# Level 5 of a blockwise inverse in 32x32 tiles of TensorE, its neighbour in column tiles, and a new order of one superstep

## The reference

```python
def step(S, inputs):
    q_t, k_t, v_t, g_t, b_t = inputs
    S = S * jnp.exp(g_t)[..., None]
    kv = jnp.einsum('bhd,bhdv->bhv', k_t, S)
    delta = b_t[..., None] * (v_t - kv)
    S = S + k_t[..., None] * delta[:, :, None, :]
    o = jnp.einsum('bhd,bhdv->bhv', q_t, S)
    return (S, o)
```

## Time and profile before

| what | value |
|---|---|
| median of 3 runs | 5065.29 us (5062.55 to 5066.39) |
| the profiled execution's own time | 5056.96 us |
| its span | 5055.0 us |
| granted TensorE clock, mean | 0.992 |
| TensorE busy | 4725.1 us (93%) |
| VectorE, ScalarE, GpSimd busy | 3754.1, 3339.2, 2881.8 us |

### The profile page before, as it was taken

The page is one execution under the profiler, slowest core; times in us unless marked ns, Lnnn a source line. Parts: engine busy times, 40 slices in busy tenths (PEclk is TensorE's granted clock), DMA queues, the critical chain, the costliest instruction groups (busy, mean ns, idle before and its releaser), DMA issues.

```text
span 5055.0 us, 111131 instructions
## 1 busy us (share of the span) xinstructions
PE 4725.1 (93%) x28928; PEld 3607.3 (71%) x28928; DVE 3754.1 (74%) x8897; ACT 3339.2 (66%) x7216; POOL 2881.8 (57%) x6210
## 2 busy tenths in 40 slices
PE   6999999999999999999999999999999997999999
PEld 4777777777777777777777777777777775555555
DVE  5878787778787778887777888777888773555555
ACT  5777777777777777777777777777777772111111
POOL 4767676667676667676667776767676761000000
PEclk8999999999999999999999999999999998999999
DMA  2211111111111111111111111111111110000000
GB/s 83 62 37 37 37 37 37 34 35 38 36 37 35 38 37 37 37 37 33 35 37 36 36 37 37 37 37 37 33 37 35 37 31 31 13 8 12 8 12 13
DMA packets 213962, 172.58 MB, mean 34 GB/s; under 512 B 146272, under 2 KB 163936, under 8 KB 213216
## 3 DMA queue, kind: packets, MB, share of 16 engines
q1 hardware_dynamic: 213344, 165.49, 11.5%
HBM read 119.03 MB, written 46.40 MB: 33 GB/s over the span
## 4 chain that ended last, share of the span: by engine, by line
PE 62%; ACT 19%; issue 11%; POOL 4%; DVE 2%; DMA 1%; POOLq 0%; SPq 0%; ACTq 0%; DVEq 0%
PE bank L1593 10%; PE bank L1384 8%; PE bank L1285 7%; PE bank L1432 4%; PE bank L1603 4%; PE bank L1406 4%; PE bank L1362 4%; ACT L642 3%; ACT lx L578 3%; PE bank L1337 2%; PE bank L1437 2%; PE bank L1293 2%; PE bank L1419 2%; ACT T L588 2%; ACT e_sb L638 2%
## 5 line engine op out<-in xcount | busy, mean ns | idle before, releaser
L1384 PE MATMUL bank<-kq,kl 128*128 128x128 f32 x6144 | 852.9, 281 | 48.2 <-DVE kq L883 40.4
L391 POOL TENSOR_TENSOR kl<-kl,tot 128x256 f32<-128x256 f32 x768 | 510.1, 664 | 565.0 <-PE bank L1384 563.7
L1384 PEld LDWEIGHTS bank<-kq,kl 128*128 128x128 f32 x6144 | 749.7, 191 | 108.9 <-issue 71.4
L1285 PE MATMUL bank<-xT,par 128*128 128x512 f32 x1536 | 750.2, 598 | 0.4 <-ACT bexp L535 0.4
L414 POOL TENSOR_TENSOR rm<-rm,mul 32x14 f32<-32x14 f32 (+6 forms) x1792 | 512.7, 286 | 141.1 <-POOL mul L410 0.8
L410 POOL TENSOR_TENSOR mul<-pm,rm 32x14 f32<-32x14 f32 (+6 forms) x1792 | 522.7, 292 | 107.4 <-issue 6.6
L883 DVE TENSOR_TENSOR kq<-kq,tot 128x512 f32<-128x512 f32 x768 | 537.4, 700 | 0.0
L893 DVE COPY_PREDICATED AT<-mask,bank 128x256 f32<-128x256 uint32 x896 | 468.0, 522 | 0.1
L371 POOL TENSOR_TENSOR rstd<-rstd,minus_half 128x4 f32<-128x4 f32 x32 | 32.3, 1008 | 738.1 <-DVE rstd L828 738.1
L801 ACT ACTIVATE q<-bank 128x512 f32<-128x512 f32 x144 | 86.0, 597 | 522.1 <-PE bank L1593 522.1
L1406 PE MATMUL bank<-T,lx 128*128 128x64 f32 x3072 | 387.1, 269 | 4.2 <-issue 4.1
(11 more groups left out here) (176 smaller groups left out, 12486.1 us busy)
## 6 DMA issues: line engine op xcount, KB each, us to landing
par<-params_dram SPq DMA_DIRECT2D x128, 519.0 KB, 3.3
blocks_out<-lx SPq DMA_DIRECT2D x128, 256.0 KB, 2.0
lx<-blocks_in SPq DMA_DIRECT2D x128, 256.0 KB, 2.7
pm<-blocks_out SPq DMA_DIRECT2D x512, 8.0 KB
blocks_in<-rm SPq DMA_DIRECT2D x512, 8.0 KB
out_dram<-xall SPq DMA_DIRECT2D x16, 512.0 KB, 2.9
xall<-x_dram SPq DMA_DIRECT2D x5, 1536.0 KB, 7.1
lx<-ffn_dram SPq DMA_DIRECT2D x1, 3456.0 KB, 11.0
```

The costliest lines, as they stand in the source:

```text
L391: pool.tensor_tensor(halves(kl[:, :], w)[:, :, 0, :], src, totr.broadcast_to([P, SEQ // (2 * w), w]), ALU.mult).then_inc(s["kl_ready"], 1)
L1285: ins = pe.matmul(bank[t][:, :], par[p][:, at:at + P], chunk(xT, kt, SEQ), start=kt == 0, stop=kt == KT - 1)
L1384: ins = pe.matmul(dst[:, :, n], chunk(left, n), right[:, :, n, :, 1, :], start=True, stop=True)
```

## The change

1. `level(5)`: for each chunk two products instead of one, each with 32 columns of weights and 64 moving columns, into the column tiles at partitions 0 and 64.
2. `lt_times_t(5)` and `t_products(5)`: for each chunk two products of 32x32 weights with 32 moving columns, in the tiles of the array that hold the two blocks.
3. `x_evict(5)` copies 128 columns instead of 256; `t_update(5)` becomes two operations on 32 partitions and 128 columns each, instead of one on 128 and 256.
4. Before each of the three tiled groups, TensorE's list has one more semaphore instruction (`pe_go`).
5. All five lists of `step` get another order. Not in the diff below: GpSimd's `next_rstd` goes behind `eliminate(iB, 3)` and `totals(7)` behind `eliminate(iB, 5)`; ScalarE's `ga_evict` goes behind `x_evict(6)`, and `w_evict(0)` ahead of `k_copy`; on VectorE `kq_init(1)` goes behind `kq_update(5)`, `qk_evict(5)` ahead of it, `next_moments` behind `l_evict(6)`, `qk_evict(6)` ahead of `t_update(6)`.

```diff
@@ -300,15 +301,14 @@
         sp.wait_ge(s["low_in"], 16 * NCH * (iB + 1))
         sp.sem_inc(s["sp_go"], 1)
-    if B:
-        next_params()
     if D:
         blocks_from_pool()
         diagonals_back()
+    next_x()
     if B:
         low_levels_out()
         blocks_to_pool()
-    next_x()
+        next_params()
 supersteps(sp, lambda bn, first: None, step)
 sp.wait_ge(s["x_mm"], HIGH * NHEAD)
...
@@ -477,18 +477,14 @@
         softplus_high()
     if B:
         kl_update(3)
+        kl_update(4)
     if A:
         totals(1)
         totals(2)
         totals(3)
         totals(4)
-    if B:
-        kl_update(4)
-    if A:
         totals(5)
         totals(6)
-        totals(7)
-    next_rstd()
     if B:
         kl_update(5)
     if C:
...
@@ -598,7 +599,8 @@
         act.wait_ge(s["x_mm"], HIGH * iD + l - LOW + 1)
         if l < LEVELS - 1:
             after(act, s["y_mm"], (HIGH - 1) * iD + l - LOW)
-            act.activation(XS, b_x[:, 0:SEQ // 2], ACT.Copy).then_inc(s["x_ev"], 1)
+            width = SEQ // 2 if l < 5 else NCH << l
+            act.activation(XS[:, 0:width], b_x[:, 0:width], ACT.Copy).then_inc(s["x_ev"], 1)
             return
         act.wait_ge(s["zero_ok"], 1)
         after(act, s["yw_mm"], iD)
...
@@ -722,42 +724,40 @@
     if A:
         tap0(1, "k_mm")
         softplus_exp()
+    if C:
+        w_evict(2)
+    if A:
         softplus_max()
         softplus_ln()
         tap0(2, "v_mm")
-    if C:
-        w_evict(2)
     if D:
         t16_scale()
-    if B:
-        lt16_scale()
-    if A:
-        decay()
     if N:
         turned_x(nb, 0)
-    if D:
-        tt16_evict()
+    if B:
+        lt16_scale()
     if C:
         w_evict(3)
     if D:
         x_evict(4)
+        tt16_evict()
+    if A:
+        decay()
     if N:
         turned_x(nb, 1)
-    if A:
-        silu(0)
-        silu(1)
     if C:
         output_squares()
     if N:
         fa_evict(nb)
+    if A:
+        silu(0)
+        silu(1)
     if D:
         tt_evict(4)
         x_evict(5)
     if A:
         silu(2)
         square(0)
-    if N:
-        ga_evict(nb)
     if B:
         turned_v()
     if A:
...
@@ -899,6 +901,14 @@
         if l < LEVELS - 1:
             tl = halves(T[:, :], w)[:, :, 0, :]
             dve.wait_ge(s["y_mm"], (HIGH - 1) * iD + l - LOW + 1)
+            if l == 5:
+                for at in (0, HALF):
+                    rows = slice(at + w, at + 2 * w)
+                    tl = T[rows, :].rearrange("p (n c) -> p n c", n=NCH)[:, :, at:at + w]
+                    ins = dve.tensor_tensor(tl, tl, b_x[rows, 256:256 + NCH * w].rearrange("p (n c) -> p n c", n=NCH),
+                                            ALU.subtract)
+                ins.then_inc(s["t_upd"], 1)
+                return
             dve.tensor_tensor(tl, tl, b_x[:, 256:512].rearrange("p (m h) -> p m h", h=w),
                               ALU.subtract).then_inc(s["t_upd"], 1)
             return
...
@@ -1030,46 +1040,41 @@
         s_update(0)
     if A:
         conv(0, 1)
+        conv(0, 2)
     if C:
         residual(1)
     if A:
-        conv(0, 2)
         conv(0, 3)
     if B:
         l_evict(1)
         qk_evict(1)
-    if A:
-        conv(1, 1)
     if C:
         s_update(1)
     if B:
         kq_update(1)
+    if C:
+        residual(2)
     if A:
         softplus_one()
         softplus_rest()
-    if B:
+        conv(1, 1)
+    if C:
+        s_update(2)
+    if B:
+        kq_update(2)
         l_evict(2)
-    if C:
-        residual(2)
-    if B:
-        kq_update(2)
         qk_evict(2)
+    if C:
+        residual(3)
     if A:
         conv(1, 2)
+    if B:
+        l_evict(3)
+        qk_evict(3)
+        kq_update(3)
+    if A:
         conv(1, 3)
-    if B:
-        l_evict(3)
-    if C:
-        s_update(2)
-    if B:
-        qk_evict(3)
-    if A:
         conv(2, 1)
-    if B:
-        kq_update(3)
-    if C:
-        residual(3)
-    next_moments()
     if B:
         l_evict(4)
         qk_evict(4)
...
@@ -1380,8 +1389,16 @@
             pe.wait_ge(s["low_done"], LOW * (iB + 1))
         right = kq[mB][:, :].rearrange("p (q n m two h) -> p q n m two h", q=2, n=NCH, two=2, h=w)
         dst = b_lvl[:, :].rearrange("p (q n m h) -> p q n m h", q=2, n=NCH, h=w)
+        if l == TILED:
+            pe.sem_inc(s["pe_go"], 1)
         for n in range(NCH):
-            ins = pe.matmul(dst[:, :, n], chunk(left, n), right[:, :, n, :, 1, :], start=True, stop=True)
+            if l != TILED:
+                ins = pe.matmul(dst[:, :, n], chunk(left, n), right[:, :, n, :, 1, :], start=True, stop=True)
+                continue
+            for m in range(HALF // w):
+                at = 2 * w * m
+                ins = pe.matmul(dst[at:at + w, :, n, m], left[:, n * P + at:n * P + at + w],
+                                right[:, :, n, m, 1, :], start=True, stop=True)
         ins.then_inc(s["lvl_mm"], 1)
     def turn_16():
...
@@ -1402,6 +1419,15 @@
         else:
             pe.wait_ge(s["t_upd"], (HIGH - 1) * iD + l - LOW)
             pe.wait_ge(s["x_ev"], HIGH * iD + l - LOW)
+        if l == 5:
+            pe.sem_inc(s["pe_go"], 1)
+            for n in range(NCH):
+                for at in (0, HALF):
+                    lo, hi = n * P + at, n * P + at + w
+                    ins = pe.matmul(b_x[at + w:at + 2 * w, n * w:(n + 1) * w], LT[l - LOW][p][at:at + w, hi:hi + w],
+                                    T[at:at + w, lo:lo + w], start=True, stop=True)
+            ins.then_inc(s["x_mm"], 1)
+            return
         for n in range(NCH):
             ins = pe.matmul(b_x[:, n * HALF:(n + 1) * HALF].rearrange("p (m h) -> p m h", h=w),
                             chunk(LT[l - LOW][p], n), halves(chunk(T, n), w)[:, :, 0, :],
...
@@ -1427,6 +1453,15 @@
             pe.wait_ge(s["tt16_ev"], iD + 1)
         else:
             pe.wait_ge(s["tt_ev"], (HIGH - 1) * iD + l - LOW)
+        if l == 5:
+            pe.sem_inc(s["pe_go"], 1)
+            for n in range(NCH):
+                for at in (w, HALF + w):
+                    hi = n * P + at
+                    ins = pe.matmul(b_x[at:at + w, 256 + n * w:256 + (n + 1) * w], TT[p][at:at + w, hi:hi + w],
+                                    XS[at:at + w, n * w:(n + 1) * w], start=True, stop=True)
+            ins.then_inc(s["y_mm"], 1)
+            return
         if l < LEVELS - 1:
             for n in range(NCH):
                 ins = pe.matmul(b_x[:, 256 + n * HALF:256 + (n + 1) * HALF], chunk(TT[p], n),
...
@@ -1481,17 +1516,18 @@
         project(0, 1)
     if C:
         state_update(0)
+        chunk_outputs(0)
     if A:
         project(1, 0)
     if C:
         k_times_s(1)
-        chunk_outputs(0)
     if B:
         level(1)
+    if A:
+        project(1, 1)
     if C:
         solve(1)
     if A:
-        project(1, 1)
         project_f()
     if C:
         state_update(1)
...
@@ -1499,33 +1535,28 @@
         k_times_s(2)
     if B:
         level(2)
+    if C:
+        solve(2)
     if A:
         project(2, 0)
+    if C:
+        state_update(2)
+        k_times_s(3)
+    if A:
         project(2, 1)
     if C:
-        solve(2)
+        chunk_outputs(2)
     if B:
         level(3)
-    if C:
-        state_update(2)
-    if A:
-        project_g(0)
-        project_g(1)
-        project_g(2)
-        project_g(3)
-    if C:
-        k_times_s(3)
+    if N:
+        turn_next_x(nb, 0)
+    if C:
+        solve(3)
     if D:
         lt_times_t(4)
-    if N:
-        turn_next_x(nb, 0)
-    if D:
         turn_16()
     if B:
         level(4)
-    if C:
-        chunk_outputs(2)
-        solve(3)
     if N:
         turn_next_x(nb, 1)
     if C:
...
@@ -1533,29 +1564,37 @@
         chunk_outputs(3)
     if D:
         t_products(4)
+    if B:
+        level(5)
+    if A:
+        project_g(0)
+        project_g(1)
+        project_g(2)
     if N:
         next_fa(nb)
-    if B:
-        level(5)
     if D:
         turn_t(4)
+    if A:
+        project_g(3)
+    if D:
         lt_times_t(5)
     if N:
         next_ga(nb)
+    if B:
+        turn_v()
     if D:
         t_products(5)
     if B:
-        turn_v()
         level(6)
     if D:
         turn_t(5)
         lt_times_t(6)
     if C:
         turn_og()
+    if A:
+        sums()
     if N:
         next_beta(nb)
-    if A:
-        sums()
     if D:
         t_products(6)
     if C:
```

More of the change, by code:

```diff
@@ L28 @@
 TURNS = (BATCH - 1) // UNROLL
+TILED = 5
 SUMS = 32
@@ L504, in step @@
                     eliminate(iB, 3)
+                next_rstd()
+                if B:
                     eliminate(iB, 4)
                     eliminate(iB, 5)
+                if A:
+                    totals(7)
+                if B:
                     eliminate(iB, 6)
@@ L767, in step @@
                     x_evict(6)
+                if N:
+                    ga_evict(nb)
                 if C:
```

32 lines of the change are left out of this document (19 added, 13 removed).

## The result

The median went from 5062.55 us (5059.44 to 5066.39, 5 runs) to **5031.44 us** (5023.64 to 5041.76, 5 runs): 0.9937 of the time, 95% interval 0.9922 to 0.9952. That is 31 us where 87.5 were forecast. The profiled execution took 5026.44 us with a span of 5024.7.

A forecast was written before the change was run, and what follows sets the result against it. TensorE, 93% busy, looked like the bound, but the superstep was read as three stretches: 13.15 + 13.1 + 0.15 + 4.38 = 30.78 us against 31.54. Taking 0.7 for 125 supersteps, 87.5 us, gave a 4977 us median, range 4930 to 5055.

The forecast's parts named there:

- stretch 2: tap0(2) to the end of square(1), ScalarE working nearly throughout: about 1.0 us shorter, 14.13 to 13.1.
- the ring: One superstep, solve(0) to solve(0), as three stretches each with its own limit: 31.54 us now, 30.78 forecast.
- stretch 1: solve(0) to tap0(2): about 0.36 us longer, 12.79 to 13.15, although level(2) starts 0.27 earlier.
- two evictions and the update: VectorE from level(4) landing to the end of kq_update(4): about 1.4 us, so level(5) starts at 2561.15.
- nobody waiting: GpSimd's totals(1) slips about 1 us behind kl_update(4), at no cost, since totals serve the next superstep.
- The tiles: nothing: Tiled level(5), lt_times_t(5), t_products(5) save 0.9 us on TensorE, but 1.3 us of pauses cover them: no gain.
- the gain of 0.7 for all 125: Every full superstep of heads 3 to 127 gains 0.7 us: 125 x 0.7 = 87.5 us in all.
- the prediction's own remark on that superstep, 1.5: Superstep that brings in a sequence might gain 1.5 us, in the rival of 4935 us; below 4930: chance 0.03.
- Tiles that serialise: No load goes under a running product in tiled groups: 1.6 us lost per superstep, 5265 us; chance 0.11.
- loads that don't overlap in level(5): level(5)'s two column tiles wait for each other's loads: 1.8 us instead of 0.65, 5065 us; chance 0.03.
- A new wait eats it: New waits at k_times_s(3) or w_evict(2) take the gain: about 5065 us, chance 0.06; small gain 0.08.

The follow-up runs named there:

- totals_wait: Changed kernel plus one GpSimd wait, so totals(1) starts only when qk_evict(4) is done; 5007.38 us, 0.9887 of the kernel before.
- order_only: The change with level(5), lt_times_t(5), t_products(5), x_evict(5) and t_update(5) in their old shape; 5117.5 us, 1.0102 of the kernel before.
- tiles_only: Kernel before with the three tiled groups, narrower x_evict(5) and two-part t_update(5), all lists in old order; 5088.61 us, ratio 1.0051.

## Why the prediction was half right

- **In short**: the way was right and the size wrong, 31 us for 87.5. In the superstep that was read, the gain was 0.43 for 0.7, because stretch 2 was mis-sized; and that superstep did not stand for all 125.
- **The bound and the ring** held. The superstep is the three stretches, and stretch 1 came out at 13.19 for 13.15: level(2) starts 2665.21 - 2663.59 = 1.62 after state_update(1), 2551.21 - 2549.59 in the forecast.
- **Stretch 2** was 0.2 too short, and the step that failed there is "two evictions and the update (0.69; about 1.4 together, an estimate)". The update took 1.13, since kl_update(4), set ahead of totals(1), makes GpSimd's next step begin a moment before it. The forecast saw that totals(1) would slip and priced it at "nobody waiting". It asked who waits for the step, and not what runs beside it at the new time. totals_wait gives the price: 0.22 of the 31.11. level(5) came 0.76 later than forecast: 0.44 is the update's length, 0.13 is level(4) landing later, and 0.19 is the hand-over from the update to the product, 0.24 (2675.67 to 2675.91) where the forecast had 0.05. That 0.24 stood in its own rows: kq_update(1) ends at 2550.55 + 0.69 = 2551.24 and level(2) starts at 2551.48.
- **"The tiles: nothing"** is the step that was wrong in kind. It took 1.3 us of pauses at t_products(5) and at sums for cover. In the changed kernel the one at sums is there (0.80), and t_products(5) starts without idle time. level(5) and lt_times_t(5) stand ahead of x_evict(5), on the chain that ScalarE waits for, with 0.6 of slack by the forecast's own times (2563.7 to 2564.3) and none in fact; the old lengths, 0.95 and 0.84 for 0.65 and 0.6, would have used up 0.54 of it by themselves. (The 0.94 that the prediction gives lt_times_t(5) is t_products(5)'s, behind a pause.) A pause covers a group only if nobody waits for that group before the pause comes. order_only shows 0.86 in place of nothing. The sum was saved by luck in another of its terms: at 0.57 and 0.37 the groups were quicker than the 0.65 and 0.6 taken.
- **GpSimd's list** was not looked at as a ring of its own. Its length from the norms to kl_update(0), 12.4 us in the median, was in the trace of before, where kl_update(0) is done 0.2 us ahead of level(1). The new order has room for it because the norms start earlier: zz comes 5.1 us ahead of sums, where tiles_only has 4.1. It still costs position 5 its 1.04: next_rstd was in the diff, and got no term.
- **The total**: the gain of 0.7 for all 125 was 0.43 where the superstep was the one read, 0.3 at position 3, -0.6 at position 5, and 1.4 at position 6 without a clock fall (the prediction's own remark on that superstep, 1.5, was nearly right). The clock falls, 10 us, stood in no rival. Of the 56 us that are missing, the smaller gain takes 125 x 0.27 = 34, position 5 takes 16, the clock falls 10 and the turns of the loop 16; position 6 gives 14 back. These are estimates from the medians, and 6 too many.
- **The rivals.** Tiles that serialise and loads that don't overlap in level(5) are refuted: its sixteen loads on the same rows of the array would take 1.8 us, and the group occupies 0.57. The Trainium skill (TensorE: Matmul & The Clock Gate, Part 3, The mechanism) states that loads overlap running products only when the row groups differ; this group does not bear that out, and the measurement decides. "A new wait eats it" named the right kind of thing and the wrong places: 0.22 of the 0.33 that the read superstep fell short went to kq_update(4), and position 5 to next_rstd.
- **Open**: the four turns of the loop over sequences. The two supersteps around one take 71 us after the change and 66 to 69 before, and TensorE's clock falls for 6.8 us in all four after, for 6.8 us in one and 3.4 us in another before. No run here was made for them, and their cause stays open.

## What to carry to other kernels

When a group of instructions is called covered, point to the pause that covers it and see that it lies behind the group and ahead of whoever waits; a pause later in the superstep covers nothing. Read each in-order list as a ring with a length of its own, the engine that is only 58% busy included: here both halves of the change lost alone because one of two rings was always full. And of a moved step ask not only who waits for it, but what it will run beside.
